# Spiking residual plus mixture of experts on one core: three shared groups ahead of the expert steps instead of four, five x1 buffers, pads cleared in two halves

## What is computed

```
c      = initial[:, None, :] + cumsum(relu(x) * 0.001, axis=time)
x1     = x + (floor(c) - previous floor) / 0.001
shared = (silu(x1 @ w1) * (x1 @ w3)) @ w2                  # 256 -> 512 -> 256, every row
s      = sigmoid([x1, cond] @ router_W)                    # 8 experts
top2   = top_k(s + router_bias, 2);  gates = s_top2 / sum(s_top2)
routed = sum over the 2 chosen e of gate_e * (gelu(x1 @ W1e[e]) @ W2e[e])
out    = x1 + (shared + routed) / 3
```

## Time and profile before

| | |
|---|---|
| median of 3 runs | 390.6 us (390.2 to 392.02) |
| the profiled execution | 392.07 us, its span 390.3 us |
| PE busy | 323.1 us (83%) |
| DVE busy | 217.7 us (56%) |
| ACT busy | 170.9 us (44%) |
| POOL busy | 148.4 us (38%) |

### The profile page before, as it was taken

The page is one execution under the profiler, slowest core; times in us unless marked ns, Lnnn a source line. Parts: engine busy times, 40 slices in busy tenths (PEclk is TensorE's granted clock), DMA queues, the critical chain, the costliest instruction groups (busy, mean ns, idle before and its releaser), DMA issues.

```text
span 390.3 us, 6873 instructions
## 1 busy us (share of the span) xinstructions
PE 323.1 (83%) x2012; PEld 290.5 (74%) x2012; DVE 217.7 (56%) x463; ACT 170.9 (44%) x285; POOL 148.4 (38%) x169
## 2 busy tenths in 40 slices
PE   0199999999967889699999299999999969797940
PEld 0078888778855889699999299999987858685730
DVE  4855869679649686679633033433322544645651
ACT  5727491673627364655556046665552112020100
POOL 2301020382777387226520000000003777777770
PEclk9998999999989698989999689999999989999995
DMA  7955064627876255436664434544322455554552
GB/s 247 290 165 144 19 163 108 161 108 191 175 179 204 92 175 178 137 106 197 196 188 151 138 100 133 152 131 137 113 98 62 134 149 162 149 157 129 163 151 73
DMA packets 38642, 57.64 MB, mean 148 GB/s; under 512 B 5200, under 2 KB 29776, under 8 KB 38608
## 3 DMA queue, kind: packets, MB, share of 16 engines
q1 hardware_dynamic: 29872, 30.98, 25.1%
q0 software_dynamic: 8736, 26.22, 24.2%
HBM read 33.07 MB, written 24.12 MB: 146 GB/s over the span
## 4 chain that ended last, share of the span: by engine, by line
PE 54%; POOL 11%; issue 10%; DMA 9%; DVE 7%; ACT 5%; SPq 2%; POOLq 0%; DVEq 0%; ACTq 0%
PE ps L1158 12%; PE ps L1159 12%; PE ps L1160 12%; POOL front L392 5%; PE ps_d L1184 4%; POOL xg L392 4%; PE ps L1317 3%; DMA xg<-y_rows,y_i 3%; PE ps_r L1202 2%; DMA w_lo<-w_all 2%; PE ps L1361 2%; PE ps_d L1317 2%; PE ps_d L1361 2%; DMA base<-w_all 2%; POOL x_slots L380 1%
## 5 line engine op out<-in xcount | busy, mean ns | idle before, releaser
L1158 PE MATMUL ps<-w_hi,parts 128*128 x288 | 89.0, 309 | 0.5 <-ACT works L646 0.4
L380 POOL DMA_INDIRECT x_slots<-base,slot_i x64 | 68.7, 1073 | 47.2 <-issue 18.7
L1159 PE MATMUL ps<-w_hi,parts 128*128 x288 | 82.8, 287 | 0.0
L1160 PE MATMUL ps<-w_lo,parts 128*128 x288 | 82.5, 287 | 0.0
L392 POOL DMA_INDIRECT xg<-y_rows,y_i x28 | 27.7, 988 | 105.2 <-issue 104.6
L1184 PE MATMUL ps_d<-w_down,works 128*128 128x256 f32 x256 | 61.0, 386 | 6.2 <-DVE works L1062 6.2
L1158 PE MATMUL ps<-x_hi,w_hi 128*128 128x512 f32 x128 | 55.2, 431 | 10.1 <-DMA w_lo<-w_all 5.8
L1184 PEld LDWEIGHTS ps_d<-w_down,works 128*128 128x128 f32 x256 | 48.7, 194 | 14.4 <-DVE works L1062 7.4
L1158 PEld LDWEIGHTS ps<-w_hi,parts 128*128 128x128 f32 x288 | 57.2, 198 | 1.0 <-issue 0.9
L1159 PEld LDWEIGHTS ps<-w_hi,parts 128*128 128x128 f32 x288 | 56.9, 197 | 0.0
L1160 PEld LDWEIGHTS ps<-w_lo,parts 128*128 128x128 f32 x288 | 56.5, 196 | 0.0
(11 more groups left out here) (127 smaller groups left out, 480.8 us busy)
## 6 DMA issues: line engine op xcount, KB each, us to landing
xg<-x_slots SPq DMA_DIRECT2D x72, 128.0 KB, 2.4
y_rows<-works SPq DMA_DIRECT2D x36, 256.0 KB, 2.4
w_lo<-w_all POOLq DMA_DIRECT2D x10, 512.0 KB, 6.1
x<-x_t SPq DMA_DIRECT2D x16, 256.0 KB, 4.5
xg<-w_all POOLq DMA_DIRECT2D x8, 512.0 KB, 6.6
out<-base SPq DMA_DIRECT2D x16, 256.0 KB, 2.4
base<-w_all SPq DMA_DIRECT2D x2, 512.0 KB, 6.9
x_slots<-zeros SPq DMA_DIRECT2D x1, 1024.0 KB, 17.4
```

Source lines behind the costliest of these rows:

```text
L380: nc.gpsimd.indirect_dma_start(x_slots, bass.IndirectOffsetOnAxis(ap=slot_i[:, k, r * RT + t:r * RT + t + 1], axis=0), base[:, rows_at(g) ...
L1158: nc.tensor.matmul(out, x_hi, w_hi, start=start, stop=False, skip_group_check=True)
L1159: nc.tensor.matmul(out, x_lo, w_hi, start=False, stop=False, skip_group_check=True)
L1160: return nc.tensor.matmul(out, x_hi, w_lo, start=False, stop=stop, skip_group_check=True)
```

## The change

PE now runs three groups of the shared network, the 36 steps, then five groups (`PRE = 3`). In detail:

- `x1k` has five buffers (`XG = 5`), so x of group 4 is loaded at once, and x of groups 5 to 7 waits for groups 0 to 2. To make room `hid` has two buffers instead of four: `hid(g, b)` is written after `down(g, b - 2)`. For the first two of group 3 a piece of `front` is used (`first_hid`).
- ACT splits the eight expert chunks in three groups instead of four. POOL corrects all of them first, and then scatters stage 0 in one go.
- The scatters of stages 1, 2 and 3 are marked to expert steps 0 to 3, 6 to 9 and 13 to 16. Before, stage 1 was marked to group 3, stage 2 to steps 2 to 5, stage 3 to steps 8 to 15.
- What ACT and PE did for the front of groups 4 and 5 beside group 3 is now beside the first expert steps, and the rest moves back by up to five steps. In the stream the list of stage 1 comes ahead of group 5's scans. The portion beside an expert step is 1.7 instead of 1.6, up to step 16 instead of 12.
- The first `up` of the first late group is cut in two: one half ahead of the last expert product, one behind; its silu is after the last copy of y.
- The eight pads are cleared in two halves of four, behind `load_tiles(18)` and `load_tiles(19)`.
- Gathers and units are shifted by a group; the third unit's gathers also wait for two `down` of group 3.

```
-    NS = NG // 2
+    PRE = 3
+    XG = 5
+    PADS = 15
...
-        works = sb("works", [P, 2 + SB, GT])
+        works = sb("works", [P, 4, GT])
...
             def load_x(g, c):
-                n = g % 4
-                if g >= 4:
-                    sp.wait_ge(s_xhi, g - 3)
+                n = g % XG
+                if g >= XG:
+                    sp.wait_ge(s_xhi, g - XG + 1)
...
-            def clear_pads():
+            def clear_pads(a):
+                sp.wait_ge(s_list, STAGES)
...
                 if s + 3 < STEPS:
                     load_tiles(s + 3)
+                if s in (PADS, PADS + 1):
+                    clear_pads(4 * (s - PADS))
...
-            def scatter(r, first=0, end=RT):
+            def scatter(r):
                 pool.wait_ge(s_slot, r + 1)
-                for t in range(first, end):
+                for t in range(RT):
                     g = (r * RT + t) // TT
-                    if r < 2:
-                        shared_step(2 + r, t)
+                    if r == 0:
+                        shared_step(2, t)
                     else:
-                        expert_step(2 + t // 2 if r == 2 else 8 + t, t % 2 == 1)
+                        expert_step((0, 0, 6, 13)[r] + t // 2, t % 2 == 1)
...
-            for k in range(SHARED_CHUNKS, SHARED_CHUNKS + 4):
-                add_w(k)
-                load_w(k + 2)
-            scatter(0, 0, 4)
-            for k in range(SHARED_CHUNKS + 4, NCHUNK):
+            for k in range(SHARED_CHUNKS, NCHUNK):
                 add_w(k)
                 if k + 2 < NCHUNK:
                     load_w(k + 2)
-                scatter(0, 4 + k - SHARED_CHUNKS - 4, 5 + k - SHARED_CHUNKS - 4)
+            scatter(0)
             for r in range(1, ROUTES):
                 scatter(r)
...
                 elif g == 2:
                     elif at == 2:
-                        split_w(6)
+                        split_w(8)
+                    elif at == 4:
+                        split_w(9)
...
-            EXPERT_FILL = (1.1, 1.6)
+            EXPERT_FILL = (1.1, 1.7)
...
                 for b in range(SB):
                     dve.wait_ge(s_act, g * SB + b + 1)
-                    after(dve, s_down, g * SB + b + 1 - SB)
+                    after(dve, s_down, g * SB + b - 1)
...
                     if s == STEPS + 2:
-                        up(NS, 0)
+                        up(PRE, 0, (0,))
                     if 3 <= s:
                         pe.wait_ge(s_ehlo, s - 2)
                         after(pe, s_ey, s - 3)
                         products(ps[3], ht_hi[(s - 3) % 2], ht_lo[(s - 3) % 2], s - 3, CC * C).then_inc(s_edn, 1)
+                    if s == STEPS + 2:
+                        up(PRE, 0, (1,))
...
-            for g in range(NS):
+            for g in range(PRE):
                 shared(g)
             experts()
             pe.wait_ge(s_ey, STEPS)
-            for g in range(NS, NG):
+            for g in range(PRE, NG):
                 shared(g)
```

More of the change, by code:

```diff
@@ L70, in build_spiking_moe @@
         w_raw_e = xg[:, :, :, :].rearrange("p (k r) u c -> p k (r u c)", k=2)
-        x1k = [sb(f"x1_{n}", [P, CC, GT]) for n in range(4)]
+        x1k = [sb(f"x1_{n}", [P, CC, GT]) for n in range(XG)]
         front = sb("front", [P, CC, 3, W])
@@ L177, in build_spiking_moe @@
         s_clc = sem("cond_logit_kept")
-        s_x = [[sem(f"x_loaded{n}_{c}") for c in range(CC)] for n in range(4)]
+        s_x = [[sem(f"x_loaded{n}_{c}") for c in range(CC)] for n in range(XG)]
         s_rate = [sem(f"rates_made{c}") for c in range(CC)]
@@ L228, in build_spiking_moe, with hid_of @@
         CONSTS, GATE_STEPS, Y_STEPS = 19, 11, 8
+        def hid_of(g, b):
+            return first_hid[:, b, :] if g == PRE and b < 2 else hid[:, b % 2, :]
         def after(engine, semaphore, value):
@@ L322, in _ @@
             sp.dma_start(rb[:, :], router_b.partition_broadcast(P)).then_inc(s_small, 16)
-            for g in range(1, 4):
+            for g in range(1, XG):
                 for c in range(CC):
@@ L328, in _ @@
                          zeros[:, :].unsqueeze(1).to_broadcast([P, E, C])).then_inc(s_dummy, 16)
-            for g in range(4, NG):
+            for g in range(XG, NG):
                 for c in range(CC):
@@ L520, in beside @@
                     elif at == 1:
+                        split_w(2)
                         make_rates(2, 0)
@@ L523, in beside @@
                     elif at == 2:
-                        split_w(2)
+                        split_w(3)
                     elif at == 3:
@@ L535, in beside @@
                         scores(0)
-                        split_w(3)
+                        split_w(4)
                         copy_rows(1, 1)
@@ L551, in beside @@
                         copy_rows(2, 0)
-                        split_w(5)
+                        split_w(7)
                         copy_rows(2, 1)
@@ L1018, in stream @@
                 yield from tile_list(0)
+                yield from tile_list(1)
                 yield from front_scans(5)
@@ L1104, in experts @@
                     if s > 0:
-                        beside(EXPERT_FILL[s < 13])
+                        beside(EXPERT_FILL[s < 17])
                     if 2 <= s:
@@ L1141, in _ @@
                 shared(g, fill_early)
-            finish(NS - 1)
+            finish(PRE - 1)
             experts()
@@ L1145, in _ @@
                 pass
-            for g in range(NS, NG):
-                if g > NS:
+            for g in range(PRE, NG):
+                if g > PRE:
                     finish(g - 1)
@@ L1165, in w_ready, with up @@
                 pe.wait_ge(s_wlo[k], 16)
-            def up(g, b):
+            def up(g, b, halves=(0, 1)):
                 after(pe, s_hid, g * SB + b - 1)
-                for half in range(2):
+                for half in halves:
                     for c in range(CC):
@@ L1175, in up @@
                                      c == 0, c == CC - 1)
-                last.then_inc(s_up, 1)
+                if 1 in halves:
+                    last.then_inc(s_up, 1)
             def down(g, b):
@@ L1264, in shared @@
                     ranks(1)
-                elif g == 3:
-                    logits(5)
                 down(g, 1)
```

197 lines of the change are left out of this document (89 added, 108 removed), and 2 rows, old and new, of the table FILL.

## The result

The changed kernel takes 404.8 us in the median of four runs (404.0 to 407.1), the kernel before 390.4 beside it (389.8 to 392.0): **1.035 times the time, 95% interval 1.031 to 1.040**. I had said 395.0, and 387.5 to 399.5 as the range. It is slower, by the two chains of scatters that I had named, and by two and a half times as much: the span grew by 11.9 us (390.3 to 402.2), not by 4.7.

A forecast was written before the change was run, and what follows sets the result against it. PE was taken to bound most of the kernel, gathers and tile waits the gaps; -5.5 + 7.2 + 1.9 - 1.9 + 3.0 = +4.7 us, put on the median of 390.6, gave about 395 us, range 387.5 to 399.5.

The forecast's parts named there:

- the two chains of scatters: Hand-over to expert steps: stage 0's scatters hold step 0, stage 1's marked scatters hold step 4, eating the end's gain; chance 0.52.
- T0: Start of expert step 0: claimed at 114.7 instead of 120.25, 5.5 us earlier, held by stage 0's scatters.
- the half wait left at step 20: PE's wait for tiles at step 20: claimed to fall from 8.11 to 3.7 us with half the pads in flight.
- the signs of being wrong: In the profile after: a first expert step before 112, no wait at step 4, or step 13 before 190.
- rival 2: Faster: steps 4 to 9 were dear through routing waits, so step 4 to 13 takes under 48, ending at 386; chance 0.18.
- T4 to T13: Start of step 4 to start of step 13: nine steps at 5.66 to 6.22 us, taken as 53.0.
- Rival 4: A stall on splits or x in groups 0 to 2 shifts everything by 2 to 5 us; chance 0.04.
- The floor of step 12: Stage 2's scatters, starting about 2 us into step 7, let step 12 start 28 to 30 us behind step 7.
- End of group 2: End of PE's groups 0 to 2 ahead of the expert steps: claimed unchanged, at about 94.5.
- T0 to T4: Start of step 0 to start of step 4: claimed 27.0 us instead of 19.8, stage 1's scatters waiting for expert products.
- T13 to T20: Start of step 13 to start of step 20: claimed 31.2 us, 27.5 of steps plus a wait of 3.7.
- The end: Last expert product to span end: claimed 98.5 us instead of 95.5, with 88.3 of PE groups and gathers hidden.

The follow-up runs named there:

- e1: The changed kernel with stage 0's scatters put back between the last weight corrections, marks kept: 396.2 us, 1.013 times the kernel before.
- e2: The changed kernel with only the marks of stage 1's scatters taken off: 398.5 us, 1.020 times the kernel before.
- e3: The changed kernel with stage 0's scatters issued once their slots are there, no marks on stages 0 and 1: 381.1 us, 0.977 times the kernel before.
- e5: e3 with the last routing stage's ranks moved to the end of step 11, ahead of step 12's wait: 378.0 us, 0.966 times the kernel before.
- e7: The changed kernel with the last routing stage's ranks moved to the end of step 11: 403.3 us, 1.029 times the kernel before.
- f1: The changed kernel with ACT's copy of group 2's first rows ahead of group 4's rounding: 400.6 us, 1.021 times the kernel before.
- f3: e5 with stage 3's marks off and pads cleared behind steps 13 and 14: 375.5 us, 0.963 times the kernel before.
- f4: f3 with the last logits ahead of stage 2's tile list and ACT's last scores in step 10: 374.2 us, 0.964 times the kernel before.
- f6: f4 with ACT's copy of group 2's first rows ahead of group 4's rounding: 368.4 us, 0.942 times the kernel before; measured first as 371.5 us.
- e6: e5 with stage 2 placed ahead of the second half of group 6's front, pads two steps earlier: 383.8 us, 0.979 times the kernel before.

## Why the prediction was right and wrong

**Right.** T0 by the scatters of stage 0 in POOL's queue; T4 by the marks of stage 1 on PE's product; gathers 1.30 us apart with five groups beside them (310.17 to 391.82 for 63 distances) and the last unit not waiting for one; the half wait left at step 20 (3.7 said, 2.9 measured); PE's 88.3 us of groups (88.2). e1, e2 and e3 take the two chains away one by one, and the time goes with them. None of the signs of being wrong came, and rival 2 (T4 to T13 under 48) is out. Rival 4 came in part, as said below.

**T4 to T13: 53.0 said, 58.0 measured.** This is the largest of the misses, though not the only one that put the result out of the range: without it 399.8 us would be left, still past 399.5. The step that failed is the analogy behind "Nine steps at 5.66 to 6.22", whose lower end comes from steps 0 to 9 of the kernel before. The first three turns of the loop do not have all products: the pipeline fills. How many they lack, the windows of the expert products alone show. First the kernel before, T0 to T9 and T4 to T13, then the changed kernel, T4 to T13 (columns: length, PE busy, weight load, DVE, ACT):

```profile
120.25:171.15 50.90, 26.67 (x168) 24.30 (x168) 10.81 (x16) 9.48 (x16) 0.87 0.42 139
140.07:187.11 47.04, 31.78 (x216) 28.74 (x216) 12.32 (x18) 10.71 (x19) 0.93 0.50 162
```

```profile
144.37:202.38 58.01, 33.39 (x216) 30.06 (x216) 11.54 (x17) 10.75 (x18) 0.91 0.39 124
```

A product is twelve matmuls: 14 products against 18, 6.7 us of PE (33.39 less 26.67). What stands beside them on PE is the same in both stretches: the rows of groups 5 to 7, the logits of groups 6 and 7, the ranks of stages 2 and 3. 50.9 + 6.7 = 57.6, and 58.0 was measured. That they come so close is partly luck, since PE also stands without work for 11.2 us and not 9.1. With the count done, the upper end, 6.22 for a step (steps 4 to 9, where the pipeline is full), was the right row, 56.0, and I had put the value half way to a wrong lower end. This is worked out from rows; no run changed the count.

By place, the 5.0 us stand close to step 12. T4 to T7 took 17.9 us, near the 17.7 of my rate; T7 to T12 took 32.4 instead of 29.4, its last 3.65 in the wait for stage 2's scatters, and step 12 took 7.8 instead of 5.9, for the last ranks are behind that wait. Against T4 to T13 of the kernel before, with the same 18 products, PE's timeline has 5.7 us without work before and 11.2 after, and some 4.5 and 8 us of logits, ranks and row transposes. That the stretch belongs to its operations and not to the hand-over is shown by its length in eleven traces with three groups ahead (the changed kernel, e1 to e5, e7, f1, f3, f4 and f6), whose T4 lies anywhere from 113.5 to 145.4: it is 58.0 to 60.3 us. Taking single waits out of it (e5, e7, f4) changed it by less than 2 us, and placing stage 2 earlier (e6) made it 65.3. Why they come to so nearly the same is open: several waits lie beside each other, and no run removed all at once.

**The floor of step 12** I put at 28 to 30 us behind T7, with the first scatter at T7 + 2. Measured: T7 + 4.7, 20.8 us to the last scatter, and T12 at T7 + 32.4. I had let it bound nothing in the sum, but in the changed kernel it binds: step 12 opens 6.9 us behind the last scatter of stage 2. With the measured start and distances T4 to T12 is 17.9 + 32.4 = 50.2, which leaves 2.8 us for step 12 in my 53.0. I had the start of the scatters 2.7 us too early and their distance at 1.31 instead of 1.39.

**End of group 2: 94.5 said, 97.1 measured.** I had put ACT's two more splits in groups 0 and 1 at nothing, "with that cover gone they would shift all by 1 to 2 us". The cover was gone in one place, and not through a split: the copy of rows stood behind a rounding for group 4 that began only at 69.21. f1 shows it: 3.7 us, some 2.8 more than the kernel before loses there. It is the fourth rival in kind, at a chance of 0.04. The delay goes on to T0, since POOL's first scatter starts at 89.3 and not 86.6; scatters 1.28 us apart and a hand-over of 7.7 us instead of 8.5 give 1.1 of it back. (In the kernel before twelve scatters, and not ten, stood ahead of the next to last weight correction.)

**T0 to T4: 27.0 us said, 28.1 measured.** The mark let the fifth scatter go 5.5 us behind T0, as said (5.7), but the eleven distances behind it took 15.6 us instead of 14.4. The section on the hardware has more on these distances.

**T13 to T20: 31.2 said, 33.5 measured.** The wait at step 20 is 0.8 us shorter than said, the seven steps take 30.6 us instead of 27.5. I had left them at the rate of the kernel before, where they had less beside them (11.42 us of DVE in its T13 to T20, 23.58 now). With the ranks and the placing of stage 3 taken forward (e7) the seven steps take 28.2, so most of it is that work beside steps 13 and 15.

**The end: 98.5 said, 95.9 measured.** PE's part was right to 0.1. The last unit's end lies 2.8 us ahead of the span's end (397.60 + 1.79 to 402.20); I had taken the 5.2 of the earlier trace rows. Why the last store takes less, no run shows. DVE's timeline:

```profile
394.56 1.29 DVE L984 SCALAR_TENSOR_TENSOR base<-ps_d,base 128x512 f32<-128x512 f32 x2 [2.70 <-PE ps_d L1171]
...
397.60 1.79 DVE L997 SCALAR_TENSOR_TENSOR base<-xg,gate,base 128x256 f32<-128x256 f32 x4
```

The misses add up: 1.6 (T0) + 1.1 + 5.0 + 2.3 + 0 - 2.6 = 7.4 us, within rounding the 7.2 between the 4.7 that I had and the 11.9 measured. The forecast was right in the two chains and in the direction; it was too low because T4 to T13 was priced too cheaply, and three smaller terms erred the same way.

## What to carry to other kernels

When a block of work is moved away from in front of a stage, list what it hid, queue by queue. Here the moved group had covered the last six scatters of stage 0 and the first eight of stage 1, and a gain only appears once their issue order and marks are moved forward as well. When a stretch is priced by analogy with another, count the big operations in both first; steps at the start of a software pipeline are cheaper than those of a full one. And where two waits lie beside each other, taking out one may give nothing until the other goes too.

## What the runs showed of the hardware

**Scatters beside long DVE operations.** Indirect DMAs are issued in 0.97 us with 0.30 between. Beside some DVE operations of 1.2 us they take 1.4 to 1.9. POOL's timeline of the changed kernel, then DVE's:

```profile
211.53 0.96 POOL L388 DMA_INDIRECT x_slots<-base,slot_i  x1 [0.30 <-issue]
212.79 1.92 POOL L388 DMA_INDIRECT x_slots<-base,slot_i  x1 [0.30 <-issue]
215.02 1.43 POOL L388 DMA_INDIRECT x_slots<-base,slot_i  x1 [0.31 <-issue]
216.75 1.43 POOL L388 DMA_INDIRECT x_slots<-base,slot_i  x1 [0.30 <-issue]
```

```profile
212.65 1.22 DVE L895 TENSOR_TENSOR front<-slot_f,turn 128x1024 f32<-128x1024 f32 x1
...
214.39 1.22 DVE L895 TENSOR_TENSOR front<-slot_f,turn 128x1024 f32<-128x1024 f32 x1
...
216.12 2.35 DVE L901 TENSOR_TENSOR front<-front,hot_s 128x1024 f32<-128x1024 f32 x2
```

The issue at 212.79, the longest of these, lies beside an operation that began 0.14 us ahead of it. The first scatter of stage 2, at 166.91 with 1.70 us, begins beside a scan of 1.22 us, and stage 2 as a whole took 20.8 us for fifteen distances, where fifteen of 1.27 are 19.1.

The fifteen traces used here, taken together, show which operations go with it, by the DVE operation that an issue overlaps longest. Of 438 issues with nothing on DVE beside them none took over 1.04 us. Beside the `TENSOR_TENSOR` above, with both inputs in SBUF, 15 took 1.68 us on average, and beside scans of 128x514 some 1.5. Beside 295 operations of 0.68 us that read one input from PSUM (`works<-works,ps`), none took over 1.04.

The Trainium skill, page "SBUF — State Buffer", section "A bandwidth-pool intuition that's wrong (but worth ruling out)", says that descriptors made by GpSimd wait until DVE releases a shared port. The rows agree in kind, an issue being longer where DVE's operation is, and not in size: the longest here is twice the usual time, not five times. This is read from traces; no run changed DVE's operations alone.
